# Softmax denominators: probabilities summed over key chunks on POOL before the product with ones, in a gated cross-attention and expert kernel

## The reference

```python
x = x + tanh(g_xattn) * xattn(layernorm(x), ctx, ctx, mask)
x = x + tanh(g_ffn) * ffn(layernorm(x))       # 8 experts, each takes the top 56 rows of a batch
# in xattn, per batch and head:
Q, K = rope(query @ Wq.T), rope(key @ Wk.T);  V = value @ Wv.T
scores = Q @ K.T / sqrt(32);  scores[mask == 0] = -inf
ctx = softmax(scores) @ V                     # out = ctx @ Wo.T
```

## Time and profile before

| | |
|---|---|
| Time, median of 3 runs | 1972.43 us (1972.38 to 1972.75) |
| Profiled execution, its own time | 1970.94 us |
| Its span, first to last instruction | 1969.3 us |
| Mean granted clock of TensorE | 0.967 of 2.4 GHz |
| Stages | context 0 to 286 us, attention 286 to 979 us, experts from 979 us |

### The profile page before, as it was taken

One profiled execution on the slowest core, in us unless ns is written; L12 is line 12 of the kernel. 1 busy time (PEld: TensorE's weight loads), 2 busy tenths in 40 slices (PEclk: granted clock), 3 DMA queues, 4 the chain that ended last, 5 costly groups with the idle time before them and its releaser, 6 DMA issues. The chain is left out here.

```text
span 1969.3 us, 31614 instructions
## 1 busy us (share of the span) xinstructions
PE 1823.8 (93%) x11654; PEld 1568.5 (80%) x11654; DVE 1021.4 (52%) x1650; ACT 717.1 (36%) x1134; POOL 212.6 (11%) x288
## 2 busy tenths in 40 slices
PE   7999974999989989999479999999999999999996
PEld 6989863776666666766279999999999999999995
DVE  6666643667556566674435354443535445354441
ACT  3232311544434344444034343343434434343340
POOL 0000001112112111120110020200202001020101
PEclk9999996999999999999679999999999999999998
DMA  5545445565554455552143353432534335353431
GB/s 221 189 184 192 165 161 137 150 149 150 124 147 133 125 145 139 139 140 72 53 143 107 107 145 107 133 117 97 152 107 138 113 101 145 104 141 116 115 107 19
DMA packets 77241, 257.47 MB, mean 131 GB/s; under 512 B 10824, under 2 KB 10824, under 8 KB 75856
## 3 DMA queue, kind: packets, MB, share of 16 engines
q1 hardware_dynamic: 65136, 221.92, 35.7%
q0 software_dynamic: 12000, 34.13, 7.5%
HBM read 193.39 MB, written 51.61 MB: 124 GB/s over the span
## 5 line engine op out<-in xcount | busy, mean ns | idle before, releaser
L1416 PE MATMUL gu_ps<-xs_hi,ws_hi 128*128 128x448 f32 x1024 | 372.7, 364 | 3.0 <-DVE xs_lo L1351 3.0
L1418 PE MATMUL gu_ps<-xs_hi,ws_lo 128*128 128x448 f32 x1024 | 372.4, 364 | 0.0
L1417 PE MATMUL gu_ps<-xs_lo,ws_hi 128*128 128x448 f32 x1024 | 370.7, 362 | 0.0
L789 DVE CUSTOM_DVE_ANT_0 junk<-m_ps,mq 112x752 f32<-112x752 f32 x256 | 236.2, 936 | 215.9 <-PE m_ps L1050 194.0
L1346 DVE TENSOR_TENSOR ws_lo<-w_raw,ws_hi 128x1024 fp32r<-128x1024 f32 x192 | 235.4, 1226 | 189.3 <-ACT ws_hi L1296 188.5
L674 ACT ACTIVATE e_t<-s_ps 125x448 f32<-125x448 f32 x384 | 201.2, 547 | 239.6 <-PE s_ps L1077 239.0
L1296 ACT ACTIVATE ws_hi<-w_raw 128x1024 fp32r<-128x1024 f32 x192 | 201.7, 1051 | 164.5 <-PE y_ps L1435 146.6
L1416 PEld LDWEIGHTS gu_ps<-xs_hi,ws_hi 128*128 128x128 f32 x1024 | 192.8, 188 | 15.0 <-issue 3.3
L1417 PEld LDWEIGHTS gu_ps<-xs_lo,ws_hi 128*128 128x128 f32 x1024 | 192.7, 188 | 13.8
L1418 PEld LDWEIGHTS gu_ps<-xs_hi,ws_lo 128*128 128x128 f32 x1024 | 192.9, 188 | 13.4
L1077 PE MATMUL s_ps<-qs,ks 128*125 128x224 f32 x768 | 199.8, 356 | 0.0
(11 more groups left out here) (133 smaller groups left out, 2553.6 us busy)
## 6 DMA issues: line engine op xcount, KB each, us to landing
w_raw<-wstream SPq DMA_DIRECT2D x192, 512.0 KB, 3.2
ks<-k_split SPq DMA_DIRECT2D x192, 188.0 KB, 3.6
k_split<-k_split SPq DMA_DIRECT2D x32, 752.0 KB, 3.5
v_rows<-v_out SPq DMA_DIRECT2D x16, 750.0 KB
vs<-v_rows SPq DMA_DIRECT2D x16, 750.0 KB
c_raw<-ctxT SPq DMA_DIRECT2D x7, 1500.0 KB, 12.8
qs<-q_hi POOLq DMA_DIRECT2D x64, 112.0 KB, 2.9
mq_raw<-maskq SPq DMA_DIRECT2D x8, 656.2 KB, 8.2
```

Of the source, the lines that this page charges most:

```text
L789: nc.vector.tensor_tensor_reduce(junk[u % 2][:].rearrange("p (a n) -> p a n", a=2), m_ps[u % 2][0:QP, :, 0:KN], mq[:, qc].rearrange("p (a ...
L1416: nc.tensor.matmul(o, w_hi[s][:, w], xs_hi[:, c], start=(c == 0), stop=False)
L1417: nc.tensor.matmul(o, w_hi[s][:, w], xs_lo[:, c], start=False, stop=False)
L1418: mm = nc.tensor.matmul(o, w_lo[s][:, w], xs_hi[:, c], start=False, stop=(c == DC - 1))
```

## The change

Each head gets a tile `e_sum` of 125 x 448 (8 of them, as of e_t). At the start of each turn t POOL runs `sum_chunks(b, t)`: it waits for the exps of head t, adds pairs 0 and 1 of e_t, waits for that, and adds pair 2. The product with ones then takes e_sum: 2 units for each quad (its two halves of 448 are the even and the odd chunks) in place of 6. A quad has 8 units, two for each of the four parts: parts 0 to 2 are the values, part 3 is the ones. Part 3 waits for `summed`, the sums of all four heads.

```diff
+        e_sum = [sb(st, f"e_sum{j}", [KP, PAIR]) for j in range(2 * HG)]
...
+        half_summed, summed = sem("half_summed"), sem("summed")
...
+                def sum_chunks(b, h):
+
+                    n, e, total = H * b + h, e_t[h % (2 * HG)], e_sum[h % (2 * HG)]
+                    if h % HG == 0:
+                        hold(pv_done, NG * b + h // HG - 1)
+                    for pc in range(KC // 2 - 2, KC // 2):
+                        hold(*exp_at(b, h, pc))
+                    nc.gpsimd.tensor_tensor(total[:], e[:, 0], e[:, 1], ALU.add).then_inc(half_summed, 1)
+                    hold(half_summed, n + 1)
+                    nc.gpsimd.tensor_tensor(total[:], total[:], e[:, 2], ALU.add).then_inc(summed, 1)
+
...
                 def body(b, j, first, last):
                     for t in range(H):
+                        sum_chunks(b, t)
                         if not first:
...
-                    for u in range(VT * part, VT * part + VT):
+                    if part == HG - 1:
+                        pe.wait_ge(summed, H * b + HG * q + HG)
+                    for u in range(2 * part, 2 * part + 2):
                         what, c = u // KC, u % KC
                         for r in range(HG):
                             h = HG * q + r
                             v = slice((h % VH) * DK, (h % VH) * DK + DK)
-                            mm = nc.tensor.matmul(o_ps[r * WAYS:r * WAYS + WAYS, what * S:what * S + S], vs[a][:, c, v] if what == 0 else ones[:],
-                                                  e_t[h % (2 * HG)][:, c // 2, c % 2 * S:c % 2 * S + S],
-                                                  start=(c == 0), stop=(c == KC - 1))
+                            o = o_ps[r * WAYS:r * WAYS + WAYS, what * S:what * S + S]
+                            if what == 0:
+                                nc.tensor.matmul(o, vs[a][:, c, v], e_t[h % (2 * HG)][:, c // 2, c % 2 * S:c % 2 * S + S],
+                                                 start=(c == 0), stop=(c == KC - 1))
+                            else:
+                                mm = nc.tensor.matmul(o, ones[:], e_sum[h % (2 * HG)][:, c * S:c * S + S], start=(c == 0), stop=(c == 1))
```

## The result

The changed kernel takes 1982.61 us (median of 6 runs, 1981.28 to 1984.69), the kernel before, run beside it, 1970.59 (6 runs). The ratio is 1.0065, with a 95% interval of 1.0051 to 1.0080: some 13 us slower, where 33 us faster was forecast. The profiled execution of the changed kernel took 1984.69 us; its span is 1983.0 us, at a mean granted clock of 0.953 against 0.967. Code lines of the two kernels differ: L1050, L1061, L1095, L988, L759, L789 of before are L1064, L1075, L1113 (values) and L1116 (ones), L1002, L773, L803 of after.

The account below looks back on a forecast made before the run. PE, filling 94% of an attention turn, was taken to set the pace: 55 us saved, less 13, 2.4, 3.0, 3.0 and 0.5, leaves 33 us, forecast 1939 us (own range 1930 to 1948; 1918 to 1960 with rivals 1 and 2).

Parts of the forecast that it names:

- The lateness of root: POOL, turns 9 to 11: root stands behind sums 9 and 10, so norm_2 begins 3.2 us late.
- the 13 and 2.4 us of the forecast: PE losses from late roots in six batches: 2.2 us each at turn 12, 0.4 us each at turn 15's second root.
- Rival 2: Root is not late, from shorter additions or DVE's slack; the 13 and 2.4 us go: 1924 us, chance 0.22.
- rival 3: POOL becomes the bound: PE's part 3 waits on summed, at 2.0 us per addition 2006 us; chance 0.09.
- rival 4: No change: PE waits elsewhere for all that it saves, 1972 us; chance 0.07.
- 13 + 2.4 + 3.0 + 3.0: Losses: two from late roots, then savings lost to DVE at turn 10 (3.0) and at turn 0 or the loop's jump (3.0).
- 0.4 + 2.2: Turns 11 and 12: wait ahead of turn 11's transpose grows from 1.3 to 1.7 us; late root costs PE 2.2 us.
- 0.4 + 0.4: Turn 1: turn 0's saved 0.43 us becomes idle time, and turn 15's second root ends some 0.4 us late.
- Rival 1: Port contention: mask behind norm_2 and one more DVE operation in turns 10 to 12 wait a full addition, 16 us: 1955; chance 0.16.
- the sign that was to show rival 1: DVE's masks or POOL's additions would show durations that spread by up to 1 us.
- 55 saved: PE: four fewer products with ones per turn, 0.43 us, over 128 turns.

Follow-up runs that it names:

- memsets: Changed kernel with each sum replaced by five chained memsets of e_sum, which read nothing; ones read pair 2 of e_t: 1986.48 us, ratio to before 1.0081.
- PE's part alone: Changed kernel without POOL's additions or the wait for them; two products with ones per head read pair 2 of e_t: 1938.3 us, ratio to before 0.9828.
- Additions: Changed kernel where POOL still sums and PE waits, but PE keeps all 48 products of a quad and nobody reads the sums: 2002.55 us, ratio 1.0157.
- the holds behind the norms: Changed kernel where POOL, behind each of the two roots, waits until DVE has done the norm before its next addition: 1967.11 us, ratio to before 0.9977.
- the order around root: Changed kernel with sums 9 and 10 put behind the first root and sum 15 behind the second: 1968.98 us, ratio to before 0.9983.
- a seventh of each addition: Changed kernel with additions over 64 of 448 columns, all instructions and waits kept; ones read pair 2 of e_t: 1930.33 us, ratio to before 0.9792.
- the best version: Changed kernel with sums 9 to 15 held behind DVE's runs of SBUF operations, all additions still made: 1949.73 us, ratio to before 0.9890.

## Why the prediction was wrong

**What held.** The additions (1156 and 1199 ns against 1.15 us), POOL's busy time (509.1 us in "500 to 520"), the group of the ones (31.5 us; 28 at full clock), and that PE never waits for summed. The lateness of root held to a third of a microsecond. The forecast counted from the scores of turn 9 at 612.85 and had root end at 621.35, 8.50 us behind them; they start at 613.49 in the kernel after, and root ends at 621.68, 8.19 us behind them. DVE waits 18.7 us for rstd in batches 1 to 6, 3.1 each, where "some 3 us" was forecast. Putting the sums behind root took that wait away and 16 us of the time with it, about the 13 and 2.4 us of the forecast. Rival 2 (root not late) and rival 3 (POOL bound) are excluded by the same rows, and rival 4 (no change) by the time. That the kernel might get slower had a chance of 0.09, for rival 3 alone.

**The first step that failed** is in the sentence "Queued behind it on DVE are the query mask and the maxima of head 0: 0.92 + 0.94 + 0.94 us". The chain was taken with durations from a trace in which POOL was nearly always idle. The sum that POOL starts behind root starts in the same moment as norm_2, and takes it from 1.00 to 2.63 us. From norm_2's start to the free buffer the forecast had 2.80 us, and 4.85 were measured (621.72 to 626.57): 1.63 are the norm, and 0.43 a gap between the mask and the maxima that need it, which a wait for PE had hidden before. The forecast had 13 + 2.4 + 3.0 + 3.0 = 21.4 us of new idle time on PE; 38.65 were measured. In the one batch shown, turns 11 and 12 have 0.4 + 1.93 + 1.57 = 3.9 us more of it, where the forecast had 0.4 + 2.2, and turn 1 has 0.53 + 1.63 = 2.2, where it had 0.4 + 0.4. Over batches 1 to 6 the waits for norm_2 and the maxima behind it come to 21.0 us, where the forecast had 13.

**The rule that was weighed, and wrongly set aside.** Rival 1 was this mechanism, with a chance of 0.16, on the ground that "only a few DVE operations are of this kind, and they would have to meet it". It was worked out for the wrong operation: the query mask keeps 932 ns in the changed kernel, since only one of its eight stands beside an addition, and it is the norm that waits. So the sign that was to show rival 1, masks or additions that spread by up to 1 us, would hardly have shown it. Twelve groups of DVE got longer in the changed kernel, the small ones among them, and they don't meet additions by chance: a sum is released by root, as the norm is, or stands waiting in POOL's queue for DVE's or ACT's next step. The price of rival 1, 16 us, is near the 17 us that the idle time was off, which is luck, since it was added up from waits that did not happen; the clock came on top. The rule of the Trainium skill ("SBUF — State Buffer", section "Who interferes with whom"), that a DVE operation with two SBUF inputs and a GpSimd one that reads SBUF exclude each other, is borne out: the router's subtraction waits beside additions and hardly beside memsets, and the maxima, which read one operand from PSUM, keep their 935 ns. The norm and the masks have one large input and were slowed by additions and somewhat by memsets, so this part does not reach them. The part of the same rule on two-port modes would. The groups before fit that: the mask passes 1500 columns in 939 ns, while operations with two large inputs take 1087 for 896 (low_q) and 936 for 752 (the maxima), half as many in a nanosecond. That the mask or the norm runs in such a mode no trace here says.

**The second step that failed** is the sum, which has no term for TensorE's clock. It stood in the prediction only as what could break it. In the account it is nearly as large as the whole idle time: unchanged products cost some 32 us more in the stage of the changed kernel. Filling the two waits of turns 11 and 12 restored the clock there and gave 6 to 8 us back, though DVE's chain, and with it the start of turn 12's scores, stayed where it was. The rest of the 32 us is put down to the clock by the profile's busy times, not by an experiment. PE's part alone shows that a share comes without additions too, 57 - 43.5 = 13.5 us less saved than the products are worth.

**The account.** Forecast for the kernel: 55 saved, 22 lost. Measured in the stage: 57 saved, 38.65 lost as idle time and some 32 as clock, which is the 14 us by which it is longer. Additions or PE's part alone give +31 and -34 us; undoing one loss at a time (the holds behind the norms, the order around root) gives 16 to 17 us each, undoing both in one gives the same 16, since the exclusion moves on to whatever is next; placing every sum of turns 9 to 15 by what DVE does gives 34.

**What stays open.** Whether the operations that were held run in a two-port mode. Why a seventh of each addition is 8 us faster than none; how much of the 32 us of clock would return if the waits at turn 1 were filled too, and which of the waits the best version still has can be taken away. The additions were not tried on another engine, nor half of them on POOL.

## What to carry to other kernels

Before work goes to an idle POOL, list the operations of DVE on the chains that PE waits for that are of the two kinds held here (tensor_scalar from SBUF to SBUF, tensor_tensor with two SBUF inputs), the tiny ones too, and price each by how long POOL works without a pause, which can be more than one instruction; then put POOL's work where DVE reads PSUM, by a wait on the last of such a run, rather than at the place where its data are ready. A place in POOL's queue counts twice: for what stands behind it there (root), and for what its end releases on both engines at once. And a saving on a PE that is 94% busy is not its busy time: where short waits came close together the clock fell, and all products behind them paid.

## What was not expected of the hardware

An operation of 112x16 elements on DVE went from 176 ns to 1164 on average, and to 1.52 us once, with a multiplication and an addition of POOL beside it; one of 112x2 went from 162 to 1687 ns, more than any one instruction of POOL beside it took. Reciprocals, statistics and reductions, which work on SBUF alone too, kept their time. DVE's busy time contains such waits: its 1650 instructions are the same, and 39 us more of it in the changed kernel are no work. Some 300 more records of products (4666 in the stage against 4360) made a kernel 6 to 8 us faster. And beside memsets of POOL, which read nothing, a two-input operation of DVE ran at its old 1086 ns, while the tensor_scalar operations did not.
